# Attention of a graph layer on one core: full matmuls and transposes rewritten as pairs over 64 rows, with the fill cut and placed anew

## The chip, the cores and the metric

The kernel runs on one core of one Trainium2 chip. The metric is the device time of one execution in microseconds. A core has five engines with a queue each: TensorE (PE; its weight loads are listed as PEld), VectorE (DVE), ScalarE (ACT), GpSimd (POOL) and the DMA queue of SyncE (SP). They meet only at semaphores.

## The reference

The input is x [32, 512, 512] and one adj [512, 512]. Everything is float32.

```python
# layer 0
x = layernorm(x + (adj @ x) @ w0 + b0)
# layer 1: 8 heads of 64, mask = adj == 0
q, k, v = split(x @ w_qkv)
attn = softmax(where(mask, -inf, q @ k.T * 64**-0.5))
o = concat(attn @ v) @ w_proj + b_proj
x = layernorm(x + (o + layernorm(o) * gamma + beta))
```

## The kernel before

To keep float32 precision, nearly every product is made of three: each operand is split into a high part (ScalarE's copy into fp32r) and a low part (VectorE's difference), and hi·hi + hi·lo + lo·hi is summed in PSUM. PSUM has eight tiles of 128 x 512 floats.

Layer 0 runs over the 32 batches first and leaves u (the normalised x) in DRAM, turned as well. Layer 1 then runs over the batches; `pe.Fori` and its like on each engine carry the batches in between, and batches 0 and 31 are written out apart, since they lack the end of a batch before or the start of one behind. A batch has 16 steps: four pairs of heads (a group of four steps each) times four blocks of 128 rows. For step k:

- `scores` (L750): for both heads a of the pair, q·k over the 64 rows of the head. These are already pairs of 64-row matmuls, one on the upper and one on the lower 64 partitions, into one PSUM tile each, three parts: six matmuls. There are two sets of two score tiles, and two steps' scores are issued together at every odd step (L855).
- `masked_max` (L991) on VectorE adds the mask, finds the row bound and writes to `probs`; `exponent` (L890) on ScalarE makes the exponentials and their sums; `inverse` (L1000) on VectorE and `normalise` (L687) on GpSimd scale the rows.
- `turn` (L767) transposes probs in TensorE, eight times 128 x 128, into two PSUM tiles (one per head, the second waited for by itself); `pt_hi_part` (L897) and `pt_lo_part` (L1004) take them out.
- after the fourth step of a group, `attend_v` (L777) makes the outputs of both heads, 16 full matmuls. `ot_halves`, `ot_sum`, `ot_hi_part` and `ot_lo_part` add the halves of the v parts and split the result one or two steps later (`output_at`, L638).

Beside this chain TensorE has "fill": 48 full matmuls of 128 rows x 512 columns per group. They are v of this batch in group 0, the output projection of the batch before in group 1, and q and k of the next batch in groups 2 and 3. Twelve of them make one unit, one PSUM tile; the units alternate between two tiles, which the outputs use as well. The fill of a group is dealt to its four steps by hand:

```python
FILL = [20, 12, 16, 0]
for k in range(STEPS):
    turn(b, k)
    if k % 2:
        for ahead in (k + 2, k + 3): scores(b, ahead)
    # then FILL[part] fill matmuls; attend_v behind the fourth step
```

The end of the batch before (bias, layernorm, gamma, residual, second layernorm, result) is dealt row block by row block over the steps by the lists `O_STEP` (statistics of o), `Z_STEP` (t = scaled o, then on GpSimd t*gamma and o+u, and one step later `add_z`: o+t) and `S_STEP` (last statistics, and one step later `result`). On GpSimd a step begins with `power`, then `normalise` of the next step, then `add_z`, then `scale_and_add`. ScalarE does the copy of one fill unit at the end of steps 0 to 2 of a group and at the head of step 3. Every queue is strictly in the written order.

## Time and profile before

| | |
|---|---|
| median of three runs | 3647.48 us (3646.90 to 3648.03) |
| profiled execution | 3647.64 us, span 3645.8 us |
| mean granted clock of TensorE | 0.995 of full speed |
| busy share PE / PEld / DVE / ACT / POOL | 98 / 79 / 76 / 61 / 51% |
| instructions | 64651, of them 18960 matmuls and transposes |

The profile is of one execution. A busy share says how long an engine had an instruction in it; TensorE's matmuls overlap, so it is the distance from one start to the next that counts, and it is read from the timeline. Layer 0 takes about the first 790 us, layer 1 the rest.

### The profile page before, as it was taken

To read this page: it belongs to the slowest core of one execution; us is meant where nothing else is said; L and a number is where in the kernel's file an instruction comes from. 1 tells how busy PE (TensorE), PEld (TensorE's weight loads), DVE (VectorE), ACT (ScalarE), POOL (GpSimd) and SP (SyncE) were. 2 spreads that over 40 slices of the span, in tenths; PEclk is the share of its full clock that TensorE was granted. 3 is DMA by queue.
4 is the path that set the end of the run, shared out by engine and by line. 5 is a ranking of instruction groups with operands and counts; after the bars stand their busy time and mean duration, and the time that the engine had idled before them with its cause. 6 is when DMAs were issued, how large, how long until landed. Compare 5 with 4: busy or idle time off the path is not lost.

```text
span 3645.8 us, 64651 instructions
## 1 busy us (share of the span) xinstructions
PE 3579.6 (98%) x18960; PEld 2872.5 (79%) x18960; DVE 2764.4 (76%) x6557; ACT 2223.4 (61%) x4629; POOL 1863.8 (51%) x2559
## 2 busy tenths in 40 slices
PE   8999999999999999999999999999999999999996
PEld 6888888877777777777777777777777777777775
DVE  7666666656778787888877778787777778787787
ACT  4444443436666666666666666666666666666664
POOL 4555555532545555555555555555555555455555
PEclk9999999999999999999999999999999999999998
DMA  6555555540111111111111111111111111111111
GB/s 196 184 184 175 170 173 176 180 141 24 56 55 51 46 46 49 46 46 46 49 46 46 46 49 46 46 46 46 46 46 47 58 48 46 46 46 46 46 54 36
DMA packets 344958, 276.19 MB, mean 76 GB/s; under 512 B 13664, under 2 KB 275808, under 8 KB 344928
## 3 DMA queue, kind: packets, MB, share of 16 engines
q1 hardware_dynamic: 344928, 275.83, 24.9%
q8 instruction: 14, 0.23, 0.0%
q14 instruction: 16, 0.13, 0.0%
HBM read 141.56 MB, written 134.22 MB: 76 GB/s over the span
## 4 chain that ended last, share of the span: by engine, by line
PE 82%; DVE 9%; ACT 4%; issue 3%; POOL 1%; SPq 0%; DMA 0%; ACTq 0%; DVEq 0%; POOLq 0%
PE bank L813 17%; PE bank L796 10%; PE bank L829 10%; PE bank L773 10%; PE bank L311 9%; PE bank L762 9%; PE bank L324 9%; PE bank L847 6%; DVE pt_lo L1010 2%; PE bank L333 1%; ACT probs L893 1%; DVE o_stats L1036 1%; DVE ot_lo L1032 1%; DVE o L1053 1%; DVE probs L996 1%
## 5 line engine op out<-in xcount | busy, mean ns | idle before, releaser
L893 ACT ACTIVATE probs<-probs,bias_row 128x512 f32<-128x512 f32 x1024 | 729.0, 713 | 488.9 <-DVE bias_row L996 488.9
L1010 DVE TENSOR_TENSOR pt_lo<-bank,pt_hi 128x512 fp32r<-128x512 f32 x1024 | 668.2, 684 | 95.1 <-ACT pt_hi L901 82.2
L695 POOL TENSOR_SCALAR probs<-probs,inv_sums 128x480 f32<-128x480 f32 (+1 forms) x1024 | 688.3, 685 | 0.0
L996 DVE CUSTOM_DVE_ANT_0 probs<-bank,mask_bias 128x512 f32<-128x512 f32 x1024 | 661.6, 684 | 0.0
L901 ACT ACTIVATE pt_hi<-bank 128x512 fp32r<-128x512 f32 x1024 | 554.9, 594 | 132.3 <-PE bank L773 129.2
L692 POOL TENSOR_TENSOR probs<-probs,inv_sums 128x32 f32<-128x32 f32 x512 | 123.8, 242 | 986.6 <-DVE inv_sums L1002 983.0
L773 PE MATMUL bank<-ident,probs 128*128 128x128 f32 x4096 | 533.9, 273 | 20.6 <-POOL probs L695 16.9
L773 PEld LDWEIGHTS bank<-ident,probs 128*128 128x128 f32 x4096 | 477.8, 140 | 90.4 <-POOL probs L695 24.6
L813 PE MATMUL bank<-x_hi,w_hi 128*128 128x512 f32 x1024 | 411.3, 402 | 16.5 <-DVE ot L1028 6.4
L813 PE MATMUL bank<-x_hi,w_lo 128*128 128x512 f32 x1024 | 412.2, 403 | 0.0
L813 PE MATMUL bank<-x_lo,w_hi 128*128 128x512 f32 x1024 | 401.3, 392 | 0.0
L701 POOL TENSOR_TENSOR o_rstd<-o_var_eps,half_neg 128x1 f32<-128x1 f32 x256 | 143.0, 558 | 299.9 <-DVE o_var_eps L1041 299.7
L796 PE MATMUL bank<-pt_hi,v 128*128 128x512 f32 x1024 | 290.9, 406 | 0.0
L1028 DVE TENSOR_TENSOR ot<-bank,ot 64x512 f32<-64x512 f32 x256 | 176.3, 689 | 146.1 <-ACT ot L921 125.4
L796 PE MATMUL bank<-pt_lo,v 128*128 128x512 f32 x1024 | 275.5, 391 | 0.0
L284 POOL TENSOR_TENSOR rstd<-var_eps,half_neg 128x1 f32<-128x1 f32 x128 | 95.9, 749 | 350.1 <-DVE var_eps L458 350.1
L378 ACT ACTIVATE u<-res,shift,rstd 128x512 f32<-128x512 f32 x128 | 104.5, 816 | 276.5 <-DVE shift L463 276.5
L813 PEld LDWEIGHTS bank<-x_hi,w_hi 128*128 128x128 f32 x1024 | 192.7, 188 | 77.5 <-DVE ot L1028 20.0
L796 PEld LDWEIGHTS bank<-pt_hi,v 128*128 128x128 f32 x1024 | 183.1, 189 | 78.7 <-issue 23.5
L813 PEld LDWEIGHTS bank<-x_hi,w_lo 128*128 128x128 f32 x1024 | 192.8, 188 | 60.2 <-issue 22.8
L442 DVE TENSOR_TENSOR yt_lo<-bank,yt_hi 128x512 fp32r<-128x512 f32 x128 | 88.4, 691 | 189.1 <-ACT yt_hi L374 189.1
L762 PE MATMUL bank<-k_hi,q_hi 64*128 64x512 f32 x1024 | 228.8, 443 | 0.0
(92 smaller groups left out, 7965.3 us busy)
## 6 DMA issues: line engine op xcount, KB each, us to landing
x_in<-in_x_dram SPq DMA_DIRECT2D x32, 1024.0 KB, 5.7
ut_hi<-ut_hi_sb SPq DMA_DIRECT2D x128, 256.0 KB, 3.5
ut_lo<-ut_lo_sb SPq DMA_DIRECT2D x128, 256.0 KB, 3.7
u_beta_rows<-ub SPq DMA_DIRECT2D x32, 1024.0 KB, 4.4
x_hi<-ut_hi SPq DMA_DIRECT2D x128, 256.0 KB, 4.3
x_lo<-ut_lo SPq DMA_DIRECT2D x128, 256.0 KB, 4.7
out_dram<-o SPq DMA_DIRECT2D x128, 256.0 KB, 3.3
ub_row<-u_beta_rows SPq DMA_DIRECT2D x124, 256.0 KB, 2.7
```

The source lines that it names most:

```text
L311: last = pe.matmul(bank[:], a[:, m, j * P:(j + 1) * P], c[:, m, :], start=n == 0, stop=n == 11)
L324: last = pe.matmul(bank[:], a[:, m, j * P:(j + 1) * P], c[:, m, :], start=m == 0 and i == 0, stop=m == 3 and i == 2)
L695: pool.tensor_scalar(probs[:, k % 2, a, cols], probs[:, k % 2, a, cols], inv_sums[:, k % 4, a:a + 1], 0.0, ALU.mult, ALU.add)\
L762: last = pe.matmul(s_bank[k % 2][a][:], l[h, pair, n * P:(n + 1) * P], r[h, pair, :], start=i == 0, stop=i == 2)
L773: last = pe.transpose(t_bank[a][:, m * P:(m + 1) * P], probs[:, k % 2, a, m * P:(m + 1) * P], ident[:])
L796: last = pe.matmul(o_bank[a][:], w, part[:, a, m, :], start=part is pt_hi and m == 0, stop=part is pt_lo and m == T - 1)
L813: last = pe.matmul(g_bank[i % 2][:], a[:, w, m, pair * P:(pair + 1) * P], c[:, m, :], start=g % 12 == 0, stop=g % 12 == 11)
L829: last = pe.matmul(g_bank[n % 2][:], a[:, m, n * P:(n + 1) * P], c[:, 2, m, :], start=g % 12 == 0, stop=g % 12 == 11)
L893: act.activation(probs[:, k % 2, a, :], probs[:, k % 2, a, :], ACT.Exp, bias=bias_row[:, k % 4, a:a + 1], scale=-1.0, accum_out=sums[:, k ...
L901: act.activation(pt_hi[:, a, :, n * P:(n + 1) * P], t_bank[a][:].rearrange("p (m n) -> p m n", m=T), ACT.Copy)\
L996: dve.tensor_tensor_reduce(probs[:, k % 2, a, :], s_bank[k % 2][a][:], mask_bias[:, k % T, :], -SCALE, 3.0e38, ALU.add, ALU.min, bias_row[ ...
L1010: dve.tensor_tensor(pt_lo[:, a, :, cols], t_bank[a][:].rearrange("p (m n) -> p m n", m=T), f32(pt_hi[:, a, :, cols]), ALU.subtract).then_i ...
```

## The change

All of TensorE's work in layer 1 is issued as pairs of matmuls over 64 rows, one on partitions 0 to 63 and one on 64 to 127, as the scores were before.

- Fill units come in twos. A sum over 128 rows is made in two runs: in run 0 the upper halves go to the first unit's tile and the lower halves to the second's; in run 1 the tiles are swapped. Between the runs TensorE waits for its own first run (`qk_half`, `v_half`, `proj_half`). The outputs of two heads are made in the same way (`pv_half`), with two fill slots between the runs.
- A turn is 16 transposes: the input is 64 rows of probs x 128 columns, the moving side a 64 x 64 identity. The upper halves go to one PSUM tile and the lower ones to the other, so both tiles hold both heads and are complete only at the end; ScalarE waits for the whole turn.
- Scores: one set of two tiles instead of two, and one step's scores in every step. The two tiles set free go, with the two that were shared, to four fill tiles, two of which are the outputs'. Outputs and fill share the pair `o_bank`.
- The fill is dealt anew: `EARLY` are slots taken out of the following group's fill (four before the fourth step's turn, two behind its scores, two between the runs of the outputs), `FILL` gives two numbers per step, before and behind the scores.
- The wait for the next turn's probs (both heads) and for the pt_lo before it stands one slot ahead of the turn.
- VectorE and ScalarE take fill units two at a time, in parts 1 and 3 (ScalarE) and 2 and 3 (VectorE); VectorE's second pt_lo waits for the scores in three of four steps; `add_z` stands ahead of `power` and `normalise` on GpSimd; the three lists of steps are new.

```diff
-            s_bank, t_bank, g_bank = (psum[0:2], psum[2:4]), psum[4:6], psum[6:8]
-            o_bank = g_bank
+            s_bank, t_bank, o_bank = psum[0:2], psum[2:4], psum[4:6]
+            g_bank = psum[6:8] + o_bank
+            TOP, BOTTOM = slice(0, HEAD), slice(HEAD, P)
...
-            O_STEP = [4, 5, 6, 7]
-            Z_STEP = [5, 7, 9, 11]
-            S_STEP = [8, 11, 12, 13]
-            FILL = [20, 12, 16, 0]
-            BEFORE = [sum(FILL[:n]) for n in range(T)]
-            assert sum(FILL) == 48
-            assert S_STEP[-1] + 2 < STEPS
+            O_STEP = [6, 7, 9, 11]
+            Z_STEP = [7, 9, 11, 12]
+            S_STEP = [9, 11, 13, 14]
+            FILL = [(4, 10), (5, 9), (5, 7)]
+            EARLY = (4, 2, 2)
+            BEFORE = [sum(EARLY) + sum(sum(f) for f in FILL[:n]) for n in range(T - 1)]
+            assert sum(EARLY) + sum(sum(f) for f in FILL) == 48
+            assert S_STEP[-1] + 1 < STEPS
+            def turned(i):
+                return t_bank[i][:].rearrange("p (a m n) -> p a m n", a=2, m=T)
+            def turned_into(rows, k, i):
+                first = k % T * P + i * HEAD
+                return rows[:, :, :, first:first + HEAD]
...
                 def batch(b, last_part=True, more=True):
                     for k in range(STEPS):
+                        if last_part and row_at(k - 1, Z_STEP) is not None:
+                            add_z(b, row_at(k - 1, Z_STEP))
                         if last_part and row_at(k - 1, S_STEP) is not None:
                             power(b, row_at(k - 1, S_STEP), 1)
                         if k + 1 < STEPS or more:
                             normalise(b, k + 1)
-                        if last_part and row_at(k - 1, Z_STEP) is not None:
-                            add_z(b, row_at(k - 1, Z_STEP))
...
-                    for a in range(2):
-                        if not (isinstance(b, int) and b * STEPS + k < 2):
-                            pe.wait_ge(max_found, b * 32 + (2 * k + a - 3))
+                    if not (isinstance(b, int) and b * STEPS + k == 0):
+                        pe.wait_ge(max_found, b * 32 + 2 * k)
                     for i, (l, r) in enumerate(parts):
                         for a in range(2):
                             h = slice(a * HEAD, (a + 1) * HEAD)
-                            last = pe.matmul(s_bank[k % 2][a][:], l[h, pair, n * P:(n + 1) * P], r[h, pair, :],
+                            last = pe.matmul(s_bank[a][:], l[h, pair, n * P:(n + 1) * P], r[h, pair, :],
                                              start=i == 0, stop=i == 2)
                             if i == 2:
                                 last.then_inc(scores_made, 1)
-                def turn(b, k):
+                def ready_to_turn(b, k):
+                    pe.wait_ge(probs_made, b * 32 + (2 * k + 2))
+                    if not (isinstance(b, int) and b * STEPS + k == 0):
+                        pe.wait_ge(ptlo_made, b * 32 + 2 * k)
+                def turn(k):
                     for a in range(2):
-                        pe.wait_ge(probs_made, b * 32 + (2 * k + a + 1))
-                        if not (isinstance(b, int) and b * STEPS + k == 0):
-                            pe.wait_ge(ptlo_made, b * 32 + (2 * k + a - 1))
                         for m in range(T):
-                            last = pe.transpose(t_bank[a][:, m * P:(m + 1) * P],
-                                                probs[:, k % 2, a, m * P:(m + 1) * P], ident[:])
-                        last.then_inc(probs_turned, 1)
-                def attend_v(b, p, last_part, more):
-                    for a in range(2):
-                        pe.wait_ge(pthi_made, b * 32 + (8 * p + 7 + a))
-                        if p == 0:
-                            if a == 0:
-                                pe.wait_ge(vlo_made, b * 4 + 4)
-                        elif p == 1 and last_part:
-                            pe.wait_ge(o_made, b * 4 + (a - 1))
-                        elif p >= 2 and more:
-                            pe.wait_ge(qklo_made, b * 8 + (4 * (p - 2) + a + 11))
-                        else:
-                            pe.wait_ge(ot_summed, b * 8 + (2 * p + a - 1))
-                        for part in (pt_hi, pt_lo):
-                            if part is pt_lo:
-                                pe.wait_ge(ptlo_made, b * 32 + (8 * p + 7 + a))
-                            for m in range(T):
-                                w = v[:, m, 2 * p + a, :, :].rearrange("p s d -> p (s d)")
-                                last = pe.matmul(o_bank[a][:], w, part[:, a, m, :],
-                                                 start=part is pt_hi and m == 0, stop=part is pt_lo and m == T - 1)
-                        last.then_inc(pv_done, 1)
-                def qk_matmuls(b, first, count, begin=False):
+                            for i, h in enumerate((TOP, BOTTOM)):
+                                cols = slice((a * T + m) * HEAD, (a * T + m + 1) * HEAD)
+                                last = pe.transpose(t_bank[i][:, cols], probs[h, k % 2, a, m * P:(m + 1) * P],
+                                                    ident[h, h])
+                                if a == 1 and m == T - 1:
+                                    last.then_inc(probs_turned, 1)
+                def attend_v(b, p, run):
+                    if run == 1:
+                        pe.wait_ge(pv_half, b * 8 + (2 * p + 2))
+                    for part in (pt_hi, pt_lo):
+                        if run == 0:
+                            pe.wait_ge(pthi_made if part is pt_hi else ptlo_made, b * 32 + (8 * p + 8))
+                        for m in range(T):
+                            first, end = part is pt_hi and m == 0, part is pt_lo and m == T - 1
+                            if run == 1 and end:
+                                if p < PAIRS - 1:
+                                    ready_to_turn(b, 4 * p + 4)
+                                elif not (isinstance(b, int) and b == B - 1):
+                                    ready_to_turn(b + 1, 0)
+                            for a, h in ((run, TOP), (1 - run, BOTTOM)):
+                                w = v[h, m, 2 * p + a, :, :].rearrange("p s d -> p (s d)")
+                                last = pe.matmul(o_bank[a][:], w, part[h, a, m, :], start=run == 0 and first,
+                                                 stop=run == 1 and end)
+                                if end:
+                                    last.then_inc(pv_done if run else pv_half, 1)
+                def half_pair(banks, left, right, run, first, end):
+                    top = pe.matmul(banks[run][:], left[run][TOP], right[run][TOP], start=run == 0 and first,
+                                    stop=run == 1 and end)
+                    bottom = pe.matmul(banks[1 - run][:], left[1 - run][BOTTOM], right[1 - run][BOTTOM],
+                                       start=run == 0 and first, stop=run == 1 and end)
+                    return top, bottom
...
+                        elif g % 12 == 0:
+                            pe.wait_ge(qk_half, b * 8 + (i + 2))
                         a, c = ((w_hi, xt_hi), (w_hi, xt_lo), (w_lo, xt_hi))[s]
-                        last = pe.matmul(g_bank[i % 2][:], a[:, w, m, pair * P:(pair + 1) * P], c[:, m, :],
-                                         start=g % 12 == 0, stop=g % 12 == 11)
+                        pair = i // 2
+                        pieces = half_pair([g_bank[i % 4], g_bank[i % 4 + 1]],
+                                           [a[:, w, m, pair * P:(pair + 1) * P] for w in range(2)], [c[:, m, :]] * 2,
+                                           run, g % 12 == 0, g % 12 == 11)
                         if g % 12 == 11:
-                            last.then_inc(qk_done, 1)
+                            for piece in pieces:
+                                piece.then_inc(qk_done if run else qk_half, 1)
...
+                    def step(k, group, part):
+                        filled = group == 0 or (last_part if group == 1 else more)
+                        begin, (front, back) = BEFORE[part], FILL[part]
+                        turn(k)
+                        fill(group, begin, front)
+                        if k + 2 < STEPS or more:
+                            scores(b, k + 2)
+                        if part < T - 2:
+                            if filled:
+                                fill(group, begin + front, back - 1)
+                            ready_to_turn(b, k + 1)
+                            if filled:
+                                fill(group, begin + front + back - 1, 1)
+                        else:
+                            fill(group, begin + front, back)
+                            fill(group + 1, 0, EARLY[0] - 1)
+                            ready_to_turn(b, k + 1)
+                            fill(group + 1, EARLY[0] - 1, 1)
+                    def last_step(k, group):
+                        turn(k)
+                        if k + 2 < STEPS or more:
+                            scores(b, k + 2)
+                        fill(group + 1, EARLY[0], EARLY[1])
+                        if group == 0:
+                            pe.wait_ge(vlo_made, b * 4 + 4)
+                        elif group == 1 and last_part:
+                            pe.wait_ge(o_made, b * 4)
                         elif group >= 2 and more:
-                            qk_matmuls(b + 1, 48 * (group - 2) + BEFORE[part], FILL[part])
-                        if part == T - 1:
-                            attend_v(b, group, last_part, more)
-                qk_matmuls(0, 0, 12, begin=True)
+                            pe.wait_ge(qklo_made, b * 8 + (4 * group + 4))
+                        else:
+                            pe.wait_ge(ot_summed, b * 8 + 2 * group)
+                        attend_v(b, group, 0)
+                        fill(group + 1, EARLY[0] + EARLY[1], EARLY[2])
+                        attend_v(b, group, 1)
...
                 def pt_hi_part(b, k):
-                    n = k % T
-                    for a in range(2):
-                        act.wait_ge(probs_turned, b * 32 + (2 * k + a + 1))
-                        act.activation(pt_hi[:, a, :, n * P:(n + 1) * P],
-                                       t_bank[a][:].rearrange("p (m n) -> p m n", m=T), ACT.Copy)\
-                            .then_inc(pthi_made, 1)
+                    act.wait_ge(probs_turned, b * 32 + (2 * k + 2))
+                    for i in range(2):
+                        act.activation(turned_into(pt_hi, k, i), turned(i), ACT.Copy).then_inc(pthi_made, 1)
...
                         if k % T == 3:
+                            unit_hi(b, k, 2, more)
                             unit_hi(b, k, 3, more)
+                        pt_hi_part(b, k)
                         if output_at(b, k, 0) and (last_part or k >= T):
                             ot_halves(*output_at(b, k, 0))
-                        pt_hi_part(b, k)
+                        if k % T == 1:
+                            unit_hi(b, k, 0, more)
+                            unit_hi(b, k, 1, more)
...
-                        if k % T < 3:
-                            unit_hi(b, k, k % T, more)
...
                 def pt_lo_part(b, k, scores_too):
-                    cols = slice(k % T * P, (k % T + 1) * P)
-                    for a in range(2):
-                        dve.wait_ge(pthi_made, b * 32 + (2 * k + a + 1))
-                        if a == 1 and scores_too:
-                            dve.wait_ge(scores_made, b * 32 + (2 * k + 6))
-                        dve.tensor_tensor(pt_lo[:, a, :, cols], t_bank[a][:].rearrange("p (m n) -> p m n", m=T),
-                                          f32(pt_hi[:, a, :, cols]), ALU.subtract).then_inc(ptlo_made, 1)
+                    for i in range(2):
+                        dve.wait_ge(pthi_made, b * 32 + (2 * k + i + 1))
+                        if i == 1 and scores_too:
+                            scores_at(b, k + 2)
+                        dve.tensor_tensor(turned_into(pt_lo, k, i), turned(i), f32(turned_into(pt_hi, k, i)),
+                                          ALU.subtract).then_inc(ptlo_made, 1)
...
+                def ot_sum(b, p, scores_of=None):
                     for a in range(2):
                         dve.wait_ge(ot_half, b * 8 + (2 * p + a + 1))
+                        if a == 1 and scores_of:
+                            scores_at(*scores_of)
...
+                        group, part = divmod(k, T)
                         ahead = k + 2 < STEPS or more
-                        if output_at(b, k, 0) and (last_part or k >= T):
-                            ot_sum(*output_at(b, k, 0))
-                        if k % T in (1, 2):
-                            unit_lo(b, k, k % T - 1, more)
-                        elif k % T == 3:
-                            unit_lo(b, k, 3, more)
-                        if last_part and k == O_STEP[3]:
-                            add_bproj(b, 3)
+                        summed = output_at(b, k, 0) and (last_part or k >= T)
                         if k + 1 < STEPS or more:
                             inverse(b, k + 1)
-                        pt_lo_part(b, k, ahead)
+                        if part >= 2:
+                            unit_lo(b, k, part * 2 - 4, last_part, more)
+                            unit_lo(b, k, part * 2 - 3, last_part, more)
+                        pt_lo_part(b, k, ahead and part != 0)
                         if last_part and row_at(k - 1, S_STEP) is not None:
                             row_shift(b, row_at(k - 1, S_STEP), 1)
                         if last_part and row_at(k, Z_STEP) is not None:
                             row_shift(b, row_at(k, Z_STEP), 0)
+                        if summed:
+                            ot_sum(*output_at(b, k, 0), scores_of=(b, k + 2) if ahead else None)
                         if ahead:
-                            masked_max(b, k + 2, waited=True)
+                            masked_max(b, k + 2, waited=part != 0 or summed)
```

## Rows read from the trace of the kernel before

**Rows 1.** the page's part 1, busy time and share of the span of each engine.

```profile
PE 3579.6 (98%) x18960; PEld 2872.5 (79%) x18960; DVE 2764.4 (76%) x6557; ACT 2223.4 (61%) x4629; POOL 1863.8 (51%) x2559
```

**Rows 2.** the page's part 4, the chain that ended last by engine.

```profile
PE 82%; DVE 9%; ACT 4%; issue 3%; POOL 1%; SPq 0%; DMA 0%; ACTq 0%; DVEq 0%; POOLq 0%
```

**Rows 3.** waits of TensorE by pair, longest first: total, times, longest us.

```profile
PE bank L773 <- POOL probs L695: 16.9, 7, 4.4
```

**Rows 4.** window of one batch: length, busy (instructions) by engine, clock, DMA.

```profile
1687.60:1775.65 88.05, 87.65 (x482) 69.87 (x482) 70.08 (x173) 59.53 (x129) 45.34 (x68) 1.00 0.16 48
```

**Rows 5.** timeline of TensorE's matmuls, one step: start, us, group.

```profile
1702.05 1.03 PE L773 MATMUL bank<-ident,probs 128*128 128x128 f32 x8
1703.02 0.50 PE L762 MATMUL bank<-k_hi,q_hi 64*128 64x512 f32 x2
1703.35 0.39 PE L762 MATMUL bank<-k_lo,q_hi 64*128 64x512 f32 x2
...
1704.28 0.40 PE L762 MATMUL bank<-k_hi,q_lo 64*128 64x512 f32 x2
1704.61 1.19 PE L796 MATMUL bank<-pt_hi,v 128*128 128x512 f32 x4
1705.64 1.08 PE L796 MATMUL bank<-pt_lo,v 128*128 128x512 f32 x4
...
1708.38 1.03 PE L773 MATMUL bank<-ident,probs 128*128 128x128 f32 x8
1709.17 0.48 PE L847 MATMUL bank<-w_hi,ot_hi 128*128 128x512 f32 x1
1709.48 0.40 PE L847 MATMUL bank<-w_lo,ot_hi 128*128 128x512 f32 x1
...
1713.57 0.39 PE L847 MATMUL bank<-w_lo,ot_hi 128*128 128x512 f32 x1
```

**Rows 6.** timeline of TensorE's weight loads in the scores.

```profile
1703.36 0.19 PEld L762 LDWEIGHTS bank<-k_hi,q_lo 64*128 64x128 f32 x2
```

**Rows 7.** timeline of ScalarE, a step with t.

```profile
1712.05 0.72 ACT L893 ACTIVATE probs<-probs,bias_row 128x512 f32<-128x512 f32 x1 [1.77 <-DVE bias_row L996]
...
1713.39 0.19 ACT L893 ACTIVATION_READ_ACCUMULATOR probs<-probs,bias_row 128x1 f32 x1
1714.44 1.09 ACT L901 ACTIVATE pt_hi<-bank 128x512 fp32r<-128x512 f32 x2 [0.86 <-PE bank L773]
1716.73 0.82 ACT L935 ACTIVATE t<-o,o_shift,o_rstd 128x512 f32<-128x512 f32 x1 [1.20 <-DVE o_shift L1046]
```

**Rows 8.** timeline of VectorE, same step and the next but two.

```profile
1711.33 0.68 DVE L996 CUSTOM_DVE_ANT_0 probs<-bank,mask_bias 128x512 f32<-128x512 f32 x1
...
1711.93 0.69 DVE L996 CUSTOM_DVE_ANT_0 probs<-bank,mask_bias 128x512 f32<-128x512 f32 x1
...
1713.27 0.69 DVE L1036 BATCH_NORM_STATS2 o_stats<-o 128x6 f32<-128x512 f32 x1
...
1715.07 1.43 DVE L1010 TENSOR_TENSOR pt_lo<-bank,pt_hi 128x512 fp32r<-128x512 f32 x2 [0.56 <-ACT pt_hi L901]
...
1728.18 1.37 DVE L1032 TENSOR_TENSOR ot_lo<-ot,ot_hi 128x512 fp32r<-128x512 f32 x1 [0.19 <-ACT ot_hi L929]
```

**Rows 9.** timeline of GpSimd, same steps.

```profile
1714.52 0.55 POOL L701 TENSOR_TENSOR o_rstd<-o_var_eps,half_neg 128x1 f32<-128x1 f32 x1 [2.78 <-DVE o_var_eps L1041]
...
1717.63 1.30 POOL L713 TENSOR_TENSOR t<-t,gamma_row 128x512 f32<-128x512 f32 x1 [1.04 <-ACT t L935]
1718.88 1.29 POOL L715 TENSOR_TENSOR o<-o,ub_row 128x512 f32<-128x512 f32 x1
...
1720.63 0.25 POOL L692 TENSOR_TENSOR probs<-probs,inv_sums 128x32 f32<-128x32 f32 x1
...
1722.16 1.31 POOL L720 TENSOR_TENSOR o<-o,t 128x512 f32<-128x512 f32 x1
...
1728.97 1.74 POOL L715 TENSOR_TENSOR o<-o,ub_row 128x512 f32<-128x512 f32 x1
```

More of the change, by code:

```diff
@@ L849, in project, with fill @@
                         if g % 12 == 11:
-                            last.then_inc(proj_done, 1)
+                            for piece in pieces:
+                                piece.then_inc(proj_done if run else proj_half, 1)
                 def batch(b, last_part=True, more=True):
-                    for k in range(STEPS):
-                        turn(b, k)
-                        if k % 2:
-                            for ahead in (k + 2, k + 3):
-                                if ahead < STEPS or more:
-                                    scores(b, ahead)
-                        group, part = divmod(k, T)
+                    def fill(group, first, count):
@@ L860, in batch @@
                         if group == 0:
[L861 removed]
+                            v_matmuls(b, first, count)
                         elif group == 1 and last_part:
[L863 to L867 removed]
```

141 lines of the change are left out of this document (85 added, 56 removed).

## The prediction, made before the changed kernel ran

> **What bounds the kernel now.** I read the page's engine shares first: TensorE is busy for 98% of the span and no other engine for more than 76% [rows 1]. The chain that ended last says the same, 82% of it TensorE [rows 2]. The waits of TensorE are next: the longest in total is 16.9 us in seven waits [rows 3], so the engine is hardly ever without data. The stretch of one batch of layer 1 is 88.05 us, with TensorE busy for 87.65, and the batch behind it has a row with the same two numbers (one of the two stands here); the clock is 1.00 there, so 2.4 GHz [rows 4]. Time can only change much in two ways: TensorE needs less for the same work, or it begins to wait.
>
> How its 88.05 us are spent is in the timeline of one step [rows 5]. A full matmul of 512 columns costs 4.09/18 = 0.227 us from start to start (1709.48 to 1713.57). A pair of 64-row matmuls costs as much as one: 0.93/4 = 0.2325 (1703.35 to 1704.28). Eight transposes cost 0.79 to the start of what follows, and 0.87 to where it really streams (its first gap is 0.31 instead of 0.23). One batch has 192 fill matmuls (v 48, output projection 48, q and k 96), 64 for the outputs, 48 score pairs and 128 transposes: 304 slots x 0.2275 = 69.2, 16 x 0.87 = 13.9, together 83.1 us. The other 4.95 us are overhead. Most of it stands around the scores. Transposes followed by scores take 0.97 + 0.33, followed by a full matmul 0.79 + 0.31: 0.20 more. From scores to full matmuls the gap is 0.33 instead of 0.23, and the next four take 1.03 instead of 0.91: 0.22 more. So a visit to 64 rows costs 0.42; a batch has eight: 3.4 us. The remaining 1.6 us are slower slots behind each visit and waits of about 1 us.
>
> **The change on TensorE, term by term.**
> (a) Mode visits. All of layer 1 is in 64-row pairs, so the eight visits go: -3.4 us a batch, and with them most of the slower slots behind them. Layer 0 stays as it is.
> (b) Slots. A fill pair needs the slot of a full matmul, and two units still take 24. I take 0.2275, the full matmul's row, since the 0.2325 of the pairs stands right behind a switch; the full matmuls behind a switch also begin slowly (4 in 1.03). Were 0.2325 lasting, 256 slots would cost 1.3 us more a batch.
> (c) Transposes. 128 full ones become 128 pairs whose moving side has 64 columns. Both weight loads of a pair start together, x2 in 0.19 us [rows 6], so I take the pair at a full transpose's 0.109. No row shows four TensorE instructions in 0.109: the transposes have two in 0.109, the scores four in 0.2325. If the latter is a limit, a pair costs 0.218, a turn 1.74 instead of 0.87 and a batch 13.9 us more. The low end is the 64 columns alone, half of 0.109: -7 us a batch. I take 0.109, the nearest row of a transpose, because the load of 128 columns stays.
> The Trainium skill ("TensorE: Matmul & The Clock Gate", Wait — 56ns, not 53.3ns?) says that with hardware decode off the sequencer spends about 62 ns on each MATMUL. By that rule a pair would take 0.124 and the turns 1.9 us a batch more, an estimate from that page; the transposes here, at one MATMUL in 0.109, don't show whether it holds.
> (d) Runs. The second run of two units waits for its first; at the unit cuts (12 and 36 of 48) scores or a turn lie between, and two fill slots (0.45) cover the outputs. Nothing, except some 0.3 us each in the last projection.
> Sum without waits: 83.1 + 0.5 for slow slots after a restart = 83.6, 4.45 us less than 88.05.
>
> **The change in the queues.** What had been covered comes due: the steps get shorter, and both halves of probs and of pt_lo are asked for one slot before the turn. I lay out TensorE per step from its turn (time 0, in us): parts 0 and 1 of a group are 0.87 + 17 slots = 4.74 and ask for probs at 4.51; part 2 is 5.19 and asks at 4.96; part 3 is 6.10 and asks for pt_hi before its outputs, at 0.87 + 5 slots = 2.01. Constants of the others, each from a row: ACT's pt_hi starts 0.2 behind the last transpose it needs (1714.44 for the turn that follows the slot of 1713.57, whose half takes 0.44), now that of the whole turn, so 1.07; the two take 1.09. A pair of exps takes 1.53 with its sums (1712.05 to 1713.39 + 0.19), t 0.82 with its successor about 0.1 earlier; two fill units, copies of the same size as pt_hi's, I put at 1.0 [rows 7]. DVE starts pt_lo 0.63 behind pt_hi, takes 0.6 for each large operation (1711.33 to 1711.93), some 1.1 for statistics (1.25 until POOL starts on them), and exp starts 0.72 behind its max [rows 7 to 9]. POOL: t*gamma 1.25, o+u 1.24 (1.74 beside DVE's ot_lo, which then takes 1.3), power 0.5, normalise 1.53 (1720.63 to 1722.16) and 0.25 behind the reciprocal, o+t 1.3 [rows 8, 9]. In parts 1 and 2 the second pt_lo also waits for the scores, ready at 2.0 + 0.9 = 2.9; single score tiles otherwise cost nothing, since max(k+1) ends before scores(k+2) start at each step I walked. A restart after a stall costs 0.11 (a first gap of 0.34).
>
> *Outputs wait for pt_hi (part 3, four a batch).* Before, six score slots with their switch lay between turn and outputs, 2.56 us, and only half a was needed. Now pt_hi is there at 2.2 and asked for at 2.0: 0.2 + 0.11 at least. In step 3 it is more: in step 2 DVE does reciprocal, two unit subtractions and pt_lo until 3.6, so exp(4) ends at 5.9, 0.6 into step 3; ACT then takes two units (1.54) before pt_hi, ready at 2.68: 0.67 + 0.11. Step 7: 0.3, and pt_lo a bit late too, 0.6 in all. Step 15: ACT is held by row 2's result ahead of exp(16), pt_hi is ready between 2.8 and 3.3: 1.0 to 1.4.
> *Rows on POOL.* `add_z` now stands ahead of `normalise`. Step 9: scores until 2.9, second pt_lo 3.5, shift, t 3.83 to 4.55, t*gamma from 4.73 to 5.98, o+u to 7.2 or 7.7; row 2's statistics come behind max(11) and ot_lo, power until 7.6 to 8.2, which is 2.8 to 3.5 of step 10. There o+t, power and normalise(11): 2.8 + 1.3 + 0.5 + 1.53 = 6.2, or 6.9; asked for at 4.96. Stall 1.3 to 1.9. Step 11 inherits: row 0's result stands ahead of exp(12), so ACT is free 1.6 into step 11, units until 2.6, pt_hi ready at 3.7 against 2.0: 1.7 to 1.85. Step 12: ACT has pt_hi, output halves (until 3.2, my estimate from pt_hi's two) and result(1), so t of row 3 starts at 3.93; POOL is through at 7.3, 2.6 of step 13; o+t 3.9, normalise(14) 5.45 against 4.51: 1.0 to 1.1. Steps 8 and 12 just make it (4.3 against 4.51).
> Sum of stalls a batch: low 0.8+0.4+1.3+1.8+1.0+1.0 = 6.3, high 0.95+0.65+2.1+2.0+1.1+1.5 = 8.3; I take 7.4, between.
>
> **The sum.** 83.6 + 7.4 = 91.0 against 88.05: +2.95 us a batch, 30 steady batches of 32: +88 us. Batches 0 and 31 lack fill, are held by the chain through max, exp and normalise in both versions, and I give them 0 (within 5 us). The profiled execution took 3647.6 us with a span of 3645.8, the median is 3647.5, so no correction: 3736 us.
>
> **Rivals.**
> *The covers hold (faster).* The stalls are only the four of 0.31 us: 83.6 + 1.2 = 84.8, -3.2 x 30 = -97: 3550 us. For it: DVE, ACT and POOL are busy 70, 60 and 45 us of 88 [rows 4], so on average there is room, and each stall gives the others time. Against it: the stalls are made of order within one or two steps, not of load. Halfway (half of my stalls, 3.7) gives 83.6 + 3.7 = 87.3, 3624 us; the sign turns at 4.45 us of stalls.
> *Turns limited by instructions.* A turn of 1.74: +13.9 a batch; the longer steps (0.87 each) swallow most stalls except those of the outputs, some 3 remaining, an estimate: 83.6 + 13.9 + 3 = 100.5, +12.4 x 30: 4020 us. For it: no row with more than four instructions in 0.23 us. Against it: loads and matmuls of a pair start within one displayed hundredth [rows 5, 6].
> *Pairs dearer by a little.* 0.2325 a slot and turns dearer in the same proportion: +1.3 + 0.3 a batch, of which the stalls take back about half: 3760 us.
> *It doesn't do what it says.* If mode switches weren't the cause of the 0.42, they would stay: 3.4 more a batch, 3840 us. The same run of transposes is followed by 0.20 less when a full matmul comes, so I give it little.
>
> **Chances.** My forecast (3650 to 3790) 0.58; covers hold, wholly or mostly (under 3640) 0.28; within 0.2% of 3647.5, which is about what a measurement of this kernel can tell from no change (7 us), 0.06; instruction-limited turns or remaining switches, over 3790, 0.08 (the dearer pairs are inside the forecast). Faster 0.28, same 0.06, slower 0.66. Range: from 3555, the end of the faster case with only the floors left, to 3790. The forecast's own range is 3700 (stalls 6.3) to 3785.
>
> **What would show it.** (a) right: no TensorE gaps of 0.33 around scores, TensorE sum per batch near 83. (c): turns of 0.87 to 0.9; at 1.0 or more it was mis-sized. Stalls: TensorE waiting for POOL's probs about 2 x 30 times, around 3 us a batch, in steps 10 and 13; for ACT's pt_hi some 4 us a batch in steps 3, 7, 11, 15. A batch under 88.05 proves the forecast wrong; if the waits of TensorE sum to less than 130 us, the walk of the queues failed; if they are near 220 and the time still fell, the slots were cheaper than I took.

## The result

The changed kernel takes 3768.84 us (median of 4, 3750.09 to 3779.40) against 3647.75 (4 runs), a ratio of 1.033 (95% interval 1.0315 to 1.0339): 121 us slower, inside the stated range and on the side forecast.

The head of the page after, its part 1, its instruction queue and the chain; they answer to [rows 1] and [rows 2]:

```profile
span 3767.2 us, 87486 instructions
...
PE 3442.6 (91%) x31248; PEld 2811.1 (75%) x31248; DVE 2750.1 (73%) x6557; ACT 2201.0 (58%) x4629; POOL 1869.5 (50%) x2559
...
q8 instruction: 58, 0.95, 0.1%
...
PE 42%; DVE 20%; ACT 19%; issue 13%; POOL 6%; ACTq 0%; DVEq 0%; DMA 0%; SPq 0%; POOLq 0%
```

TensorE's share fell from 98 to 91%, though its matmuls and transposes rose from 18960 to 31248 and the program's instructions by a third. Of the chain it holds 42% instead of 82: DVE and ACT have 39% now. The waits of TensorE, total, times and longest [rows 3]; "issue" is time in which the profile shows nothing that it waits for:

```profile
PE bank L817 <- ACT pt_hi L990: 102.8, 95, 2.0
PE bank L824 <- POOL probs L713: 74.5, 60, 1.9
PE bank L824 <- DVE k_lo L1104: 40.6, 30, 1.4
PE bank L817 <- DVE o L1143: 27.9, 31, 1.4
PE bank L796 <- issue: 18.3, 4, 4.9
```

One batch of layer 1 [rows 4], then four single steps: step 14 at two granted clocks (in two batches), step 10 and step 13. Behind the five busy times stands the granted clock:

```profile
1714.54:1804.43 89.89, 82.31 (x866) 66.22 (x864) 69.59 (x172) 58.81 (x128) 45.54 (x69) 0.98 0.15 46
1973.76:1980.24 6.48, 6.48 (x57) 5.35 (x55) 4.57 (x12) 2.77 (x6) 2.07 (x4) 0.74 0.00 0
1792.37:1797.25 4.88, 4.88 (x56) 4.06 (x54) 4.31 (x12) 2.50 (x5) 2.08 (x4) 1.00 0.00 0
1765.92:1773.33 7.41, 5.48 (x56) 3.93 (x54) 6.95 (x18) 3.62 (x9) 6.80 (x8) 0.99 0.13 35
1785.74:1792.37 6.63, 4.73 (x52) 3.83 (x50) 5.20 (x15) 5.66 (x14) 5.85 (x6) 1.00 0.00 0
```

The batch shown took 89.89 us, and TensorE is busy for 82.3 of it instead of 87.7. It is one of the eight shortest of the thirty steady batches (89.88 to 89.93); their mean is 91.8 (88.05 before), since in the others the clock falls or TensorE waits for "issue" (below). TensorE's matmuls in a step without a wait [rows 5]:

```profile
1714.54 0.66 PE L796 MATMUL bank<-ident,probs 64*128 64x64 f32 x16
1715.00 0.47 PE L824 MATMUL bank<-w_hi,x_lo 64*128 64x512 f32 x1
...
1715.31 0.38 PE L824 MATMUL bank<-w_hi,x_hi 64*128 64x512 f32 x1
...
1716.01 0.39 PE L780 MATMUL bank<-k_hi,q_hi 64*128 64x512 f32 x2
1716.23 0.40 PE L780 MATMUL bank<-k_lo,q_hi 64*128 64x512 f32 x2
...
1718.74 0.39 PE L824 MATMUL bank<-w_hi,x_hi 64*128 64x512 f32 x1
...
1718.97 0.65 PE L796 MATMUL bank<-ident,probs 64*128 64x64 f32 x16
```

A turn costs 0.46 to the next start, 0.54 with the late first fill slot (0.31 for 0.227); nothing is lost around the scores; 15 slots from 1715.31 to 1718.74 take 3.43, 0.2287 each. In the later slots it is 0.2267. The steps in us from turn to turn (median over batches; from the starts of the turns in the traces):

| step | 0 | 1 | 2 | 3 | 4 | 5 | 6 | 7 | 8 | 9 | 10 | 11 | 12 | 13 | 14 | 15 |
|---|---|---|---|---|---|---|---|---|---|---|---|---|---|---|---|---|
| before | 5.47 | 5.42 | 4.52 | 6.33 | 5.43 | 5.42 | 4.52 | 6.33 | 5.92 | 5.42 | 5.01 | 6.33 | 5.68 | 5.42 | 4.52 | 6.33 |
| predicted | 4.74 | 4.74 | 5.19 | 7.0 | 4.74 | 4.74 | 5.19 | 6.6 | 4.74 | 4.74 | 6.9 | 8.0 | 4.74 | 5.8 | 5.19 | 7.35 |
| after | 4.43 | 4.46 | 4.88 | 7.61 | 4.43 | 4.46 | 4.88 | 7.30 | 4.47 | 4.43 | 7.42 | 7.99 | 4.45 | 6.63 | 6.47 | 7.17 |
| g1 (below) | 4.43 | 4.46 | 4.88 | 7.10 | 4.43 | 4.46 | 4.88 | 6.57 | 4.46 | 4.43 | 7.56 | 7.92 | 4.46 | 6.62 | 4.89 | 7.19 |

("predicted" is the prediction's layout plus the middle of each stall's range.) Without waits the batch would be (4.43 + 4.45 + 4.88 + 5.79) x 4 = 78.2 us, an estimate; 5.79 is 23 slots and a turn of 0.57, and no step of that kind ran without a stall. So 9.8 us a batch were gained on TensorE and 13.6 lost: 11.7 in the stalls of the shortest batches (89.9 - 78.2), 1.9 on average by the clock and by "issue".

The longest wait is not always the one that sets a step's length. In step 10 TensorE waits twice:

```profile
1771.40 0.49 PE L824 MATMUL bank<-x_hi,w_hi 64*128 64x512 f32 x1 [1.34 <-DVE k_lo L1104]
...
1772.95 0.58 PE L824 MATMUL bank<-x_hi,w_hi 64*128 64x512 f32 x1 [0.59 <-POOL probs L713]
```

The 30 waits for k_lo (40.6 us above) are fill that waits for its tiles, and they end before the probs come: by these rows TensorE would have stood at the second wait instead, had they been shorter.

### The profile page after: what moved, and what is told of

It is laid out like the page before. It is cut to its first block, busy times and chain, and to the rows that moved or that the text cites. A ratio compares the mean times of both kernels' runs of the same rounds, so it can differ in the third digit from the quotient of the medians.

```text
span 3767.2 us, 87486 instructions
## 1 busy us (share of the span) xinstructions
PE 3442.6 (91%) x31248; PEld 2811.1 (75%) x31248; DVE 2750.1 (73%) x6557; ACT 2201.0 (58%) x4629; POOL 1869.5 (50%) x2559
## 4 chain that ended last, share of the span: by engine, by line
PE 42%; DVE 20%; ACT 19%; issue 13%; POOL 6%; ACTq 0%; DVEq 0%; DMA 0%; SPq 0%; POOLq 0%
PE bank L817 14%; PE bank L311 9%; PE bank L324 8%; DVE pt_lo L1098 7%; ACT pt_hi L990 6%; ACT probs L983 5%; PE bank L824 4%; DVE probs L1082 4%; DVE ot L1118 3%; PE bank L796 3%; DVE o_stats L1126 2%; POOL probs L713 2%; ACT v L999 2%; PE bank L333 1%; DVE o L1143 1%
## 5 line engine op out<-in xcount | busy, mean ns | idle before, releaser
L824 PE MATMUL bank<-x_hi,w_hi 64*128 64x512 f32 x1024 | 422.6, 413 | 60.9 <-DVE k_lo L1104 40.6
L824 PE MATMUL bank<-x_hi,w_lo 64*128 64x512 f32 x1024 | 415.2, 405 | 56.9 <-POOL probs L713 56.9
L826 PE MATMUL bank<-x_hi,w_hi 64*128 64x512 f32 x1024 | 422.7, 413 | 0.0
L796 PEld LDWEIGHTS bank<-ident,probs 64*128 64x128 f32 x8192 | 350.7, 142 | 96.3 <-issue 24.1
L817 PE MATMUL bank<-pt_hi,v 64*128 64x512 f32 x2048 | 299.0, 409 | 131.0 <-ACT pt_hi L990 102.8
L826 PE MATMUL bank<-x_lo,w_hi 64*128 64x512 f32 x1024 | 415.2, 405 | 0.0
L824 PE MATMUL bank<-x_lo,w_hi 64*128 64x512 f32 x1024 | 415.2, 405 | 0.0
L826 PE MATMUL bank<-x_hi,w_lo 64*128 64x512 f32 x1024 | 415.2, 405 | 0.0
L796 PE MATMUL bank<-ident,probs 64*128 64x64 f32 x8192 | 351.0, 226 | 37.0 <-issue 18.3
L817 PEld LDWEIGHTS bank<-pt_hi,v 64*128 64x128 f32 x2048 | 195.4, 188 | 215.4 <-DVE k_lo L1104 84.5
L817 PE MATMUL bank<-pt_lo,v 64*128 64x512 f32 x2048 | 291.9, 401 | 0.0
L824 PEld LDWEIGHTS bank<-x_hi,w_hi 64*128 64x128 f32 x1024 | 195.3, 191 | 120.4 <-DVE k_lo L1104 53.3
L824 PEld LDWEIGHTS bank<-x_hi,w_lo 64*128 64x128 f32 x1024 | 196.0, 191 | 97.1 <-POOL probs L713 69.5
```

Source lines behind the costliest of these rows:

```text
L796: last = pe.transpose(t_bank[i][:, cols], probs[h, k % 2, a, m * P:(m + 1) * P], ident[h, h])
L817: last = pe.matmul(o_bank[a][:], w, part[h, a, m, :], start=run == 0 and first, stop=run == 1 and end)
L824: top = pe.matmul(banks[run][:], left[run][TOP], right[run][TOP], start=run == 0 and first, stop=run == 1 and end)
L826: bottom = pe.matmul(banks[1 - run][:], left[1 - run][BOTTOM], right[1 - run][BOTTOM], start=run == 0 and first, stop=run == 1 and end)
```

## The experiments

Each ratio below is to the kernel before on the same chip, with its 95% interval. The diffs are abridged: `...` stands for lines and arguments left out. The steps named are medians over the thirty steady batches of the one traced execution.

**e1: GpSimd's order of before.**

```diff
@@ pool batch
-                        add_z(...)
                         power(...)
                         normalise(b, k + 1)
+                        add_z(...)
```

> The changed kernel with GpSimd's order of before: power, normalise, then add_z. My theory: the stalls of steps 10 and 13 are a normalise that stands behind o+t. In step 10 normalise(11) starts when VectorE's reciprocal lets it (4.4 instead of 5.5), which takes 1.1 us from that stall; in step 13 it starts 1.3 us earlier. About 2.4 us a batch, and perhaps 1 more where the clock no longer falls to 1.2 GHz in step 14: 3670 to 3700 us against 3769. Rival (VectorE's statistics set normalise, GpSimd's order is nothing): within 10 us of 3769.

3747.55 us (3742.74 to 3773.46), 1.027 (1.0255 to 1.0289): 21 us less, between theory and rival. Step 13 does fall by 1.6 us to 5.03. But in step 10 the gain is 0.3 (7.12). `power` waits there for statistics that VectorE ends at 4.2, so normalise starts at 4.8 instead of 5.4 and not at 4.4, and then TensorE waits last for VectorE (turn at 1758.90):

```profile
1764.43 0.49 PE L824 MATMUL bank<-x_hi,w_hi 64*128 64x512 f32 x1 [1.40 <-DVE k_lo L1104]
...
1765.72 0.71 PE L824 MATMUL bank<-x_hi,w_hi 64*128 64x512 f32 x1 [0.33 <-DVE pt_lo L1098]
```

Step 15 grows from 7.17 to 8.32: the last statistics wait for the later o+t and end 2.5 us into step 14 instead of at 0.1, and the inverse, the unit subtractions and the exps behind them come late. The traced execution, the slowest of the five, also has six waits for "issue" (26.2 us). GpSimd in step 10 of the changed kernel (turn at 1765.92, the next at 1773.33):

```profile
1766.09 1.29 POOL L731 TENSOR_TENSOR t<-t,gamma_row 128x512 f32<-128x512 f32 x1 [1.02 <-ACT t L1019]
1767.33 1.76 POOL L733 TENSOR_TENSOR o<-o,ub_row 128x512 f32<-128x512 f32 x1
1769.09 0.55 POOL L719 TENSOR_TENSOR o_rstd<-o_var_eps,half_neg 128x1 f32<-128x1 f32 x1
1769.60 1.27 POOL L738 TENSOR_TENSOR o<-o,t 128x512 f32<-128x512 f32 x1
1770.83 0.55 POOL L719 TENSOR_TENSOR o_rstd<-o_var_eps,half_neg 128x1 f32<-128x1 f32 x1
1771.34 0.24 POOL L710 TENSOR_TENSOR probs<-probs,inv_sums 128x32 f32<-128x32 f32 x1
1771.56 1.34 POOL L713 TENSOR_SCALAR probs<-probs,inv_sums 128x480 f32<-128x480 f32 x2
```

This is the row that the prediction walked, o+u with 1.76 beside ot_lo included [rows 9]: o+u until 3.2, power, o+t, power, normalise from 5.4 to 7.0 of the step; the walk had it end at 6.2 or 6.9.

**e2: result behind the exps.**

```diff
@@ act batch
-                            result(b, row_at(k - 1, S_STEP))
                             ...
                             exponent(b, k + 2)
+                            result(b, row_at(k - 1, S_STEP))
```

> The changed kernel with ScalarE's result() moved behind the exps of the same step. My theory: in steps 10 and 14 the result (0.82 us) delays exp and through it pt_hi of steps 11 and 15, for which TensorE waits ahead of the outputs: 0.7 us less in each of these two steps, 1.4 a batch, 3720 to 3735 us. Rival (VectorE's subtractions of the fill units set the outputs' start, not ScalarE): 3760 to 3769.

3844.89 us, 1.055 (1.0513 to 1.0582): 76 us more, against theory and rival. In the changed kernel result runs while ScalarE waits for the max anyway (6.8 to 7.6 of step 10, its max comes at 7.4), which I had read as a delay. Behind the exps it stands ahead of the unit copies of step 11 and delays pt_hi by 0.6: step 11 grows to 8.6, and to near 10 in 14 of 30 batches; step 15 grows to at least 8.9, and past 10 in 24; the mean clock is 0.959.

**e3: fill and outputs as full matmuls, same places.**

```diff
 def half_pair(banks, left, right, run, first, end):
-    top = pe.matmul(banks[run][:], left[run][TOP], right[run][TOP], ...)
-    bottom = pe.matmul(banks[1 - run][:], left[1 - run][BOTTOM], ...)
-    return top, bottom
+    return (pe.matmul(banks[run][:], left[run], right[run], start=first, stop=end),)
```

> The changed kernel with fill and outputs as full 128-row matmuls again, one unit per run, in the same places of the schedule; turns and scores stay pairs, and the waits between runs are gone. By (a) of the prediction each visit to 64 rows costs 0.42 us; a group has seven of them now (turn and scores apart in three steps, together in the fourth), 28 a batch, 11.8 us of TensorE. Theory: the stalls, 13.6 us a batch, lie in a few steps and take up a third of that: 3950 to 4050 us. Rival (the pairs bring nothing, the stalls hide all of it): 3769 or less.

3826.48 us (3825.80 to 3827.16), 1.049 (1.0476 to 1.0511): 58 us more than the changed kernel, less than my 180 to 280. The price of a visit is confirmed: steps 0, 1 and 2 are 5.15, 5.19 and 5.61, about 0.73 longer each for two visits, 0.36 a visit. TensorE in one of them (columns as in [rows 5]):

```profile
1740.07 0.39 PE L820 MATMUL bank<-w_hi,x_lo 128*128 128x512 f32 x1
1740.39 0.50 PE L780 MATMUL bank<-k_hi,q_hi 64*128 64x512 f32 x2
1740.73 0.39 PE L780 MATMUL bank<-k_lo,q_hi 64*128 64x512 f32 x2
...
1741.29 0.50 PE L820 MATMUL bank<-w_hi,x_hi 128*128 128x512 f32 x1
1741.62 0.40 PE L820 MATMUL bank<-w_lo,x_hi 128*128 128x512 f32 x1
```

The gaps of 0.32 to 0.34 are back before and behind 1740.39 and 1741.29. But the waits take up more than I thought: steps 3, 7, 11 and 15 shrink to 6.74, 6.30, 7.96 and 6.93, step 10 to 6.89, step 13 to 5.54. Step 14 is 5.61 in every batch, since the clock falls only outside the steady batches. Of 28 x 0.36 = 10.1 us a batch 1.6 arrive (93.4 against 91.8), or 3.5 when the shortest batches of the changed kernel (89.9) are compared, in which the clock holds in step 14 as well.

**e4, e5, e6: which work makes the stalls.** e4 runs GpSimd's t*gamma, o+u and o+t on 64 columns; e5 does the copy and subtraction of fill units 2 and 3 on 64 columns; e6 both. The other columns are left out, so these three do not compute the reference's result. For example:

```diff
-        pool.tensor_tensor(o[:, n, :], o[:, n, :], t[:], ALU.add)
+        pool.tensor_tensor(o[:, n, 0:64], o[:, n, 0:64], t[:, 0:64], ALU.add)
```

> The changed kernel with GpSimd's three row operations (t*gamma, o+u, o+t) on 64 of the 512 columns only; the rest of the residual and of the scaled row is left out. Theory: GpSimd's row work is what makes the stalls of steps 10 and 13 and with them the fall of the clock: 2.5 + 2.2 us shrink to under 1.5 together, and step 14 loses its 1 us: 3640 to 3670 us. Rival (the waits for pt_hi and the units ahead of the outputs dominate, and other steps' stalls grow in their place): above 3720.

> The changed kernel; the copy and the subtraction of fill units 2 and 3 of each group (v, q, k and the bias add of the projection) take 64 of 512 columns, the rest of these units is left stale. Theory: in each fourth step TensorE waits ahead of the outputs for ScalarE, which does two unit copies before pt_hi, and for VectorE, which does two unit subtractions: 0.8 us less in each of the four steps, 3.2 a batch: 3660 to 3680 us against 3769. Rival (what is taken off there comes back as a wait for probs in the next steps): above 3740.

> e5_short_units and e4_short_rows together (row operations of GpSimd and units 2 and 3 on 64 columns). Theory: the two kinds of stall add up: e5's 3.2 us a batch come off e4's 3689: about 3590 us, under the kernel before. Rival (one chain behind both): no less than 3660.

e4: 3689.32 us, 1.015 (1.0099 to 1.0196), between theory and rival. Step 13 has no stall left (4.43) and step 10 is 6.44, but 11 and 15 are 8.3 instead of 8.0 and 7.2: a third comes back ahead of the outputs. e5: 3696.74, 1.014 (1.0121 to 1.0155): steps 3, 7, 11 and 15 are 6.77, 6.64, 7.18 and 6.34, 0.7 to 0.8 less each, as forecast, the rest is as it was, and the total comes 17 us above my band. e6: 3575.95, 0.981 (0.9785 to 0.9825): 193 us under the changed kernel where the two alone give 80 and 72, so they add up, and more. With this work away the new form is the faster one by 2%, so it isn't TensorE that loses. The same cut was not made in the kernel before; TensorE is busy there for all but 0.4 us of a batch, so little could be won by it.

**g1: unit subtractions ahead of inverse in the third step** (the order of before there).

```diff
@@ dve batch
+                        if part == 2:
+                            unit_lo(0), unit_lo(1)
                         inverse(b, k + 1)
-                        if part >= 2:
+                        if part == 3:
                             unit_lo(...), unit_lo(...)
```

> The changed kernel with VectorE's order of before in the third step of a group: the two fill-unit subtractions ahead of inverse() instead of behind it. In the trace inverse waits there for the exps until 1.36 us into the step, and the subtractions, whose data lie ready from the step's start, take 1.2 us behind it. Theory: max(k+2) and so the exps of the fourth step's start come 0.9 us earlier, ScalarE reaches pt_hi that much earlier, and TensorE's wait ahead of the outputs shrinks by 0.7 to 0.9 in each of the four last steps: about 3.3 us a batch, 3655 to 3680 us against 3769. Rival (ScalarE's two unit copies ahead of pt_hi set it, not the exps): 3750 or more.

3678.71 us (3675.16 to 3681.21), 1.008 (1.0065 to 1.0099): 90 us less, as the theory had it in total, but for other reasons. Steps 3 and 7 lose 0.5 and 0.7, steps 11 and 15 nothing: 36 us. The rest is not in the theory. Step 14 is 4.89 in 28 of 30 batches, where the changed kernel had about 6.47 in 20 (29 us), and no steady batch has a wait for "issue" (18 us). The chain of the changed kernel through steps 2 and 3 (start, us; turn at 1728.31):

```profile
1724.78 0.07 DVE inv_sums L1088
...
1726.10 1.28 DVE pt_lo L1098 x2
1727.38 0.60 DVE probs L1082
...
1729.54 0.96 ACT v L999 x2
1730.50 0.99 ACT pt_hi L990 x2
...
1731.62 2.16 PE bank L817 x16
```

VectorE waits for the exps until 1724.78, does two units and pt_lo, then the max; the exps end in step 3, two unit copies and pt_hi follow, and TensorE stands for 1.45 us until 1731.62. VectorE's own row of that max, and then VectorE in step 2 of g1 (turns at 1723.42 and at 1703.66):

```profile
1727.29 0.68 DVE L1082 CUSTOM_DVE_ANT_0 probs<-bank,mask_bias 128x512 f32<-128x512 f32 x1
...
1704.56 1.28 DVE L1109 TENSOR_TENSOR v<-bank,v 128x512 fp32r<-128x512 f32 x2
1705.76 0.15 DVE L1088 RECIPROCAL inv_sums<-sums 128x2 f32<-128x2 f32 x1
1705.83 1.27 DVE L1098 TENSOR_TENSOR pt_lo<-bank,pt_hi 128x512 fp32r<-128x512 f32 x2
1707.02 0.68 DVE L1082 CUSTOM_DVE_ANT_0 probs<-bank,mask_bias 128x512 f32<-128x512 f32 x1
```

The units fill the time before the inverse, and the max stands 3.36 behind the turn instead of 3.87.

**g2, g3.** g2 is g1 with e1's order; g3 is g1 with the last statistics of row block 0 a step earlier:

```diff
-            S_STEP = [9, 11, 13, 14]
+            S_STEP = [8, 11, 13, 14]
```

> g1_units_first and e1_addz_behind together. Theory: with VectorE no longer late, normalise in step 10 can use its earlier place, and e1's gain, 20 us alone, comes out larger: 60 us under g1, 3600 to 3620. Rival (step 10's reciprocal stands behind two statistics as before, so e1 keeps its 20): 3640 to 3660.

> g1_units_first with the last statistics of row block 0 in step 8 instead of 9 (S_STEP[0] = 8), GpSimd's order as changed. Theory: in step 10 the reciprocal waited until 4.1 behind ot_lo and two statistics; one less frees it 1.1 us earlier, but GpSimd's o+t and power still hold normalise until about 4.9 instead of 5.5: 0.6 us a batch, 20 us under g1. Rival (the clock's fall to 1.2 GHz in step 14 hangs on the length of step 10's stall and goes with it): 50 us or more under g1.

3689.58 (1.011, 1.0093 to 1.0127) and 3689.33 (1.012, 1.0103 to 1.0137): 11 us above g1 each, against both theories. In g2 step 13 falls to 5.02, but 14 and 15 grow to 5.82 and 7.92, and three waits for "issue" (13.5 us) fall into the traced execution. In g3 step 11 falls from 7.92 to 7.30 and step 10 stays as it was (7.57 against 7.56). g3's median steps sum to 0.6 less than g1's, but its step 14 runs in part at 1.2 GHz in 11 of 30 batches against 2 (mean 5.44 against 4.99), which takes nearly all of it back; the mean clock is 0.982 against 0.989. Why the clock falls there again stays open.

**h1, h2, h3: the turn alone, in the kernel before.** `turn` and the two layouts that go with it are changed, in odd steps (h1, scores follow there, so no visit is added), in all (h2), in the second step of each group (h3). The waits are the same in the three and differ from those of before: every step asks for the next probs one slot ahead of the turn, and the outputs wait for both halves of pt_hi.

```diff
 # pe, before.py
+    for i, h in enumerate((TOP, BOTTOM)):
+        pe.transpose(t_bank[i][:, cols], probs[h, k % 2, a, m * P:(m + 1) * P], ident[h, h])
```

> The kernel before, with the turns of odd steps as 16 transposes of 64 rows (the change's turn alone); scores follow these turns, so no visit to 64 rows is added. The wait for probs stands one slot ahead of the turn. Theory: a turn in pairs takes 0.50 us instead of 0.87 (the changed kernel's trace) and all covers of the kernel before stay: 8 x 0.37 = 3.0 us a batch of 32, 3555 to 3575 us against 3647. Rival (the short turn in the changed kernel is a gain that the waits for both halves of pt_hi give back here too, ahead of the outputs): 3630 to 3650.

> The same with all 16 turns of a batch in pairs; the even ones stand between full matmuls, so eight visits to 64 rows come back. Theory: a visit costs 0.36 to 0.42 us and the pair turn saves 0.37: within 15 us of h1_odd_turns. Rival (a visit costs nothing when a turn makes it, the cost before was the scores'): another 90 us less, 3470 to 3490.

> The kernel before with turns in pairs in the second step of each group only (h1_odd_turns has them in the fourth too, where the outputs then wait for both halves of pt_hi). In h1's trace the second steps are 0.47 us shorter each, the fourth ones by 0.09 on average while the steps behind them grow. Theory: the fourth steps give nothing because the outputs wait for pt_hi there: 4 x 0.47 = 1.9 us a batch, of which the fill's waits for k_lo and the output sums give back about 0.9 as in h1: 3600 to 3625 us, a little under h1's 3627. Rival (the waits of the fill take back all that the second steps gain; h1's rest came from the fourth steps): 3630 to 3647.

h1: 3626.74 us (3624.72 to 3632.40), 0.994 (0.9926 to 0.9959), the fastest version here that computes everything; 52 us above the theory's band and 3 under the rival's. Steps 1, 5, 9 and 13 are 4.95 instead of 5.42, but of the 3.0 us a batch only 0.6 arrive (87.44 against 88.05). The rest comes back, most of it as waits that were none, 5.7 and 6.4 us in the kernel before:

```profile
PE bank L829 <- ACT pt_hi L940: 27.5, 61, 1.2
PE bank L846 <- DVE k_lo L1052: 20.0, 30, 0.7
...
PE bank L846 <- DVE ot L1064: 18.1, 30, 0.6
```

h2: 3641.32, 0.998 (0.9975 to 0.9994), 15 us above h1, as forecast: a visit costs about what the pair turn saves. h3: 3634.88 (3634.30 to 3638.05), 0.9965 (0.9951 to 0.9978), within the rival's band, not mine: the fourth steps do carry 8 us of h1's gain.

## Why the prediction was right

The direction and the mechanism held: TensorE got shorter and began to wait, in the steps named. The waits for probs came as forecast (60 times, 74.5 us), those for pt_hi a little shorter (102.8 us); not forecast were the 27.9 us of step 7, where VectorE's o ends the wait, and the 40.6 for k_lo in step 10. By its own steps:

- (a) *Mode visits.* Right. They are gone after; e3 prices one at 0.36, h2 against h1 at about a turn's saving; predicted 0.42.
- (b) *Slots.* Right: 0.2267 in the long runs.
- (c) *Transposes.* Mis-sized. A turn costs 0.54, not 0.87; pairs start 0.06 apart, close to the low end of the bounds (half of 0.109). I had taken the load of 128 columns for the limit. A step without a wait is 0.31 shorter than laid out (4.43 for 4.74), which makes 16 x 0.31 = 5.0 us a batch. The figure weighed there (62 ns for each MATMUL with hardware decode off; the Trainium skill, "TensorE: Matmul & The Clock Gate", Wait — 56ns, not 53.3ns?) does not bound these turns: sixteen transposes start in 0.46 us, 29 ns each. Whether hardware decode was on, no run here shows.
- (d) *Runs.* Right: no wait between the runs in the steady batches.
- *Stalls.* Each named stall is there and most are larger: 1.8, 1.5, 2.5, 2.2, 2.2 and 1.4 in steps 3, 7, 10, 11, 13, 15 against 0.8 to 0.95, 0.4 to 0.65, 1.3 to 2.1, 1.8 to 2.0, 1.0 to 1.1 and 1.0 to 1.5. The sum, 11.6, is 4.2 above my 7.4, nearly the 5.0 by which the turns were cheaper. In steps 11 and 15 the length came out as laid out (7.99 and 7.17 for 8.0 and 7.35), so what the turns saved there became stall; in 3, 7, 10 and 13 it came out 0.5 to 0.8 longer. So two errors cancelled, in part by a mechanism: where a stall ends is a matter of the other queues' chain, and what TensorE saves ahead of it becomes stall. e3 shows the same from the other side (10.1 us more work, 1.6 to 3.5 more time). That they cancelled so nearly is luck.
- *What the walk missed.* The shortest batches, 89.9 us, are what the walked mechanism makes: +1.85 us a batch or +55 us, where I had +88. Another 57 us (the mean of 91.79 against 89.9) come from two things that the prediction does not mention; counted one by one below they give 62. The clock: in 20 of 30 steady batches step 14 runs in part at 1.2 GHz (the window with 0.74: 6.48 us instead of 4.88), after the stall of step 13, 20 x 1.6 = 32 us; three steps 11 and the start of four batches add some 12. And waits for "issue": four steps 15 are 4 to 5 us longer by them, 18 us by the waits above. The end, batch 31 and the last rows, took 11 us more where I had 0. That the total lies so near the forecast is luck in this part.
- *Step 3* was short by 0.6 in the walk. The exps end 6.1 us behind the turn of step 2, where I had 5.9, and step 2 is 0.31 shorter, so pt_hi is ready 3.2 us into step 3 instead of 2.68. g1 shows that the order of the unit subtractions and the inverse is worth 0.5 us of step 3.

The sum: 91.79 - 88.05 = 3.74, x 30 = 112, and 11 at the end, less 2 at the start, is 121; forecast +88.

## What to carry to other kernels

When the work of the engine that bounds a kernel gets 10% shorter, walk the other queues over a whole period first: the length of a stalled step is set by their chain, and most of what is saved ahead of the stall becomes stall. Read from the trace which wait ends last in a step, not which is longest. Put work whose data lie ready (a unit's subtraction, a result) where its engine waits anyway, and try both orders on the chip; three of my five reorderings went against my own walk. A cheaper piece can pay alone: the 64-row turn where scores follow gained 0.6% in the kernel that still had its covers.

## What the runs showed of the hardware that I had not expected

- Two 64-row transposes of 128 x 64 run side by side every 0.06 us, twice the rate of the full ones (0.109).
- The granted clock falls from 2.4 to 1.2 GHz and comes back within a step, behind steps in which TensorE stood for about 2 us each (5.48 of 7.41 and 4.73 of 6.63 us busy), with single waits of at most 2.0 us. The length of these stalls alone does not decide it: in g1 steps 10 and 13 are as long (7.56 and 6.62), and step 14 stays at 2.4 GHz in 28 of 30 batches. What does is open.
- The kernels with 87486 instructions move more packets in the instruction queue: 22 to 103, against 14 to 17 in those with 65 to 72 thousand, and TensorE shows waits of up to 4.9 us for "issue" at a batch's first turn in the former alone. The two go together: 22 packets and no such wait in g1, 31 and one in g3 and e6, 40 and two in e4, 49 and three in g2, 58 and four in the changed kernel, 76 and six in e1 and e2, 103 and nine in e5, so nine packets for each wait. In the changed kernel each of the four waits begins within 1 us of the first of its nine packets, which spread over that batch. It looks like code that is fetched again; no run here tried it, and why it falls into some batches only is open. The times of these kernels scatter more, too (3750 to 3779, against 3825.8 to 3827.2 for e3).
